# Row maxima in two halves, residual sums ahead of the layer norm, and gated products on GpSimd

## The reference, cut to what matters

```
gate  = q . mean(k of a chunk of 32 tokens); own chunk always, later chunks never
sel   = the 4 best chunks for each token and head
p     = softmax(q.k / sqrt(8)) over the keys of selected chunks, causal
o     = p @ v ;  o * rsqrt(mean(o*o) + 1e-6) * weight * sigmoid(x @ Wg1.T @ Wg2.T)
x1    = layernorm(x + o @ Wo.T)
z     = 2*x1 + shared experts(x1) + sum over 16 experts of gate * (relu(x1@w1+b1) @ w2 + b2)
out   = layernorm(z)
```

## Time and profile before

| | |
|---|---|
| median of 3 runs | 1453.98 us (1453.93 to 1454.67) |
| the profiled execution | 1453.75 us |
| its span, first to last instruction | 1451.7 us |
| PE busy | 1332.4 us, 92% of the span |
| DVE busy | 1087.7 us, 75% |
| ACT busy | 842.7 us, 58% |
| POOL busy | 533.9 us, 37% |

### The profile page before, as it was taken

One profiled execution on the slowest core, in us unless ns is written; L12 is line 12 of the kernel. 1 busy time (PEld: TensorE's weight loads), 2 busy tenths in 40 slices (PEclk: granted clock), 3 DMA queues, 4 the chain that ended last, 5 costly groups with the idle time before them and its releaser, 6 DMA issues.

```text
span 1451.7 us, 29057 instructions
## 1 busy us (share of the span) xinstructions
PE 1332.4 (92%) x10992; PEld 738.7 (51%) x10992; DVE 1087.7 (75%) x2747; ACT 842.7 (58%) x1266; POOL 533.9 (37%) x638
## 2 busy tenths in 40 slices
PE   5677999999998999999999999989999899999597
PEld 3422475535754366534755356543665347553364
DVE  6994688957897578966889578975889668885434
ACT  5406774396735876277743967358762877439121
POOL 3203542254323642245422553235432454225143
PEclk8667999999999999999999999999999999999799
DMA  6001022200321021210222003210112102220031
GB/s 243 16 15 17 16 79 76 52 17 16 104 66 38 30 59 60 74 31 16 82 71 55 16 17 102 71 33 30 60 62 71 31 16 68 73 53 23 13 113 58
DMA packets 52283, 77.81 MB, mean 54 GB/s; under 512 B 6334, under 2 KB 26800, under 8 KB 51888
## 3 DMA queue, kind: packets, MB, share of 16 engines
q1 hardware_dynamic: 52144, 75.96, 18.0%
HBM read 67.02 MB, written 8.65 MB: 52 GB/s over the span
## 4 chain that ended last, share of the span: by engine, by line
PE 61%; DVE 19%; ACT 11%; DVEq 3%; issue 3%; DMA 2%; POOL 1%; SPq 0%; POOLq 0%
PE PS L562 14%; PE PS L574 13%; PE PS L718 8%; ACT UQ L992 7%; PE PS L492 7%; PE PS L509 3%; DVE hr L1163 3%; ACT UK L992 2%; DVE CM L1356 2%; DVEq L1155 2%; PE PS L773 2%; PE PS L413 2%; DVE CM L1275 2%; PE PS L728 2%; PE PS L483 2%
## 5 line engine op out<-in xcount | busy, mean ns | idle before, releaser
L1051 POOL TENSOR_TENSOR hp<-hr,hp 128x512 f16<-128x512 f32 (+1 forms) x200 | 237.1, 1186 | 584.1 <-ACT hp L849 520.0
L1356 DVE TENSOR_REDUCE CM<-PS 128x32 f32<-128x1024 f32 x320 | 376.2, 1218 | 23.2 <-PE PS L492 18.9
L574 PE MATMUL PS<-W,hp 128*128 128x256 f16 (+1 forms) x2400 | 323.2, 274 | 4.6 <-POOL hp L1051 3.6
L562 PE MATMUL PS<-x1T,W 128*128 128x512 f16 (+1 forms) x1200 | 320.6, 385 | 0.0
L840 ACT ACTIVATE hr<-PS,CF 128x512 f32<-128x512 f32 (+1 forms) x200 | 137.2, 686 | 234.3 <-PE PS L562 234.3
L574 PEld LDWEIGHTS PS<-W,hp 128*128 128x128 f16 (+1 forms) x2400 | 216.9, 98 | 96.1 <-issue 34.7
L849 ACT ACTIVATE hp<-hr 128x512 f16<-128x512 f32 (+1 forms) x178 | 112.5, 632 | 169.3 <-DVE hr L1163 156.2
L1163 DVE TENSOR_TENSOR hr<-hr,gB 128x512 f32<-128x512 f32 x176 | 126.2, 717 | 64.9 <-ACT hr L840 58.5
L992 ACT ACTIVATE UK<-PS 128x1024 f32<-128x1024 f32 x160 | 153.0, 1037 | 11.4 <-PE PS L509 11.0
L562 PEld LDWEIGHTS PS<-x1T,W 128*128 128x128 f16 (+1 forms) x1200 | 107.7, 100 | 100.7 <-issue 34.9
L992 ACT ACTIVATE UQ<-PS 128x1024 f32<-128x1024 f32 x160 | 150.9, 1041 | 3.1 <-PE PS L509 1.4
(11 more groups left out here) (150 smaller groups left out, 1793.8 us busy)
## 6 DMA issues: line engine op xcount, KB each, us to landing
gB<-gates SPq DMA_DIRECT2D x64, 256.0 KB, 3.3
gB<-gates SPq DMA_DIRECT2D x32, 224.0 KB, 2.9
gB<-gates SPq DMA_DIRECT2D x32, 192.0 KB, 2.9
gB<-gates SPq DMA_DIRECT2D x32, 160.0 KB, 2.6
xT<-in_xT SPq DMA_DIRECT2D x8, 512.0 KB, 5.8
qET<-rows SPq DMA_DIRECT2D x16, 256.0 KB, 5.2
v<-in_x SPq DMA_DIRECT2D x8, 512.0 KB, 4.1
gB<-gates SPq DMA_DIRECT2D x32, 128.0 KB, 2.9
```

The source lines that it names most:

```text
L562: mm = pe.matmul(PS[0:w, BK_H[c % 2], :], W1[:, a, k, bass.ds(f0, w)], x1T[:, e, k, :], start=(n == 0), stop=(n == 5))
L574: mm = pe.matmul(PS[:, BK_Y + j // 2, (j % 2) * D:(j % 2 + 1) * D], hp[0:w, slot, a, j * P:(j + 1) * P], W2[0:w, e, bass.ds(c, 1), :].rear ...
L1051: nc.gpsimd.tensor_tensor(hp[0:w, slot, 1, :], hr[0:w, slot, :], hp[0:w, slot, 0, :], ALU.subtract).then_inc(pool_hp, 1)
L1356: nc.vector.tensor_reduce(dst, src, AX.X, ALU.max).then_inc(dve_cm, 1)
```

## The change

1. Chunks. The maxima stage takes chunks 11 to 23 and the `up` of chunk 24 (`DEALT` has 91 pieces); the transition as a block of its own is gone. The parts of `down` for chunks 22 (three of four), 23 and 24 stand among the first nine units of the probability stage.
2. Gated products of chunks 11 to 23 are done by POOL, just ahead of its `low`. Chunk 24's relu, gated product and high part are done by DVE after the maxima stage; its `low` stands inside POOL's first causal group.
3. The biased maxima are made in two halves of 16 heads. The first half's four tiles are made in the maxima stage (after the reductions of units 21, 24, 27 and 30), transposed by PE in unit 34, scaled by ACT. The second half's follow after chunk 24's steps on DVE; PE transposes them after unit 8 of the probability stage and DVE scales them.
4. The transfers of selection rows and maxima rows are in two halves too. Unit 0 waits for the first half, unit 20 for the second. The first half is issued by SP ahead of the gate transfer of chunk 24.
5. The output gate's matmuls and tanh stand in the maxima stage, at chunks 14 and 15.
6. Bank pair 2 is first used by unit 10 in place of unit 5, and only after the residual sums have been read; the order of pairs then is 2, 0, 1 throughout.
7. On DVE: scaling of the second maxima, residual sums, copy of the outputs of group 0, then the whole layer norm, without the copy inside.

```
-PAIRS = ((0, 1, 0, 1, 0), (2, 1, 0, 2, 1), (0, 1, 2, 0, 1), (2, 0, 1, 2, 1))
-C_FIRST, C_TOPK, C_MAX, C_BIAS = (0, 3), (3, 11), (11, 22), (22, 25)
+PAIRS = [n % 2 if n < 2 * NU else (2, 0, 1)[(n - 2 * NU) % 3] for n in range(TU)]
+BACK = [next((k for k in range(1, n + 1) if PAIRS[n - k] == PAIRS[n]), 0) for n in range(TU)]
+C_FIRST, C_TOPK, C_MAX, C_LATE = (0, 3), (3, 11), (11, 24), (24, 25)
-DEALT += [(MC - 2, 4), (MC - 2, 5), (MC - 2, 6)]
+DEALT += [(MC, 0), (MC, 1), (MC, 2)]
+AT_SEL, AT_GATE, AT_NEG = (1, 2), (3, 4), 11
...
# SP, in spread_gates(m), for chunk c
+                    if m < B - 1 and c == NC - 1:
+                        bias_rows(m + 1, 0)
...
# PE, after the 40 max units
+                pe.wait_ge(s_rows[0], 64 * (b + 1))
+                unit(0, 0)
+                unit(0, 1)
+                late_down(NC - 3, (1,))
+                unit(0, 2)
+                late_down(NC - 3, (2, 3))
+                unit(0, 3)
+                late_down(NC - 2, (0, 1))
+                unit(0, 4)
+                late_down(NC - 2, (2, 3))
+                unit(1, 0)
+                if m is not None:
+                    pe.wait_ge(s_hid, (m + 1) * NC + 2)
+                outputs(0, 0, 0)
+                unit(1, 1)
+                late_down(NC - 1, (0, 1))
+                unit(1, 2)
+                outputs(0, 0, 1)
+                late_down(NC - 1, (2, 3))
+                unit(1, 3)
+                maxima_rows(BK_H[1], 1)
+                outputs(0, 0, 2)
+                unit(1, 4)
+                outputs(0, 0, 3)
...
# POOL, maxima stage
+                    for c in range(*C_MAX):
+                        gated(m, c, c % 2)
                         low(m, c, c % 2)
...
# DVE
+                        if u in FREE:
+                            maxima(FREE.index(u), 0)
...
+                    nc.vector.tensor_scalar(hr[:, s_last, :], PS[:, BK_H[s_last], :], b1[:, NC - 1:NC], 0.0, ALU.add,
+                                            ALU.max).then_inc(s_hid, 1)
+                    dve.drain()
+                    gated(m, NC - 1, s_last, split=True)
                 for j in range(NT):
+                    maxima(j, 1)
+                dve.wait_ge(pe_neg, 2 * b + 2)
+                nc.vector.tensor_scalar(negT[:, 1, :], PS[0:HALF, BK_H[1], :], 1.0 / UNIT, None, ALU.mult).then_inc(dve_neg, 1)
...
                 if m is not None:
-                    finish(m, lambda: copy_outputs(0))
-                else:
-                    copy_outputs(0)
+                    residual(m)
+                copy_outputs(0)
+                if m is not None:
+                    finish(m)
```

More of the change, by code:

```diff
@@ L98 @@
 UNITS2 = struct.unpack("f", struct.pack("ee", UNIT, UNIT))[0]
+FREE = [u for u in range(TU // 2, MU) if all(part != 2 for _, part in dealt(u - 1))][0:2 * NT:2]
 def gate_pieces(c):
@@ L257, in build @@
         act_neg = sem("act_neg")
-        s_rows = sem("s_rows")
+        dve_neg = sem("dve_neg")
+        s_rows = [sem(f"s_rows{n}") for n in range(2)]
         pe_g1 = sem("pe_g1")
@@ L706, in unit, with late_down @@
+                def late_down(c, parts):
+                    for j in parts if m is not None else ():
+                        down(m, c, c % 2, j)
+                def unit(g, d):
+                    n = g * NU + d
+                    if n < RING:
+                        pe.wait_ge(dve_cm, (b + 1) * TU + n + 1)
+                    if BACK[n]:
+                        pe.wait_ge(act_p, b * TU + n + 1 + RING - BACK[n])
+                    if n == 2 * NU and m is not None:
                         pe.wait_ge(dve_z, 2 * m + 3)
-                    key_unit(g, PAIRS[gs][d], d)
+                    if n == TU // 2:
+                        pe.wait_ge(s_rows[1], 64 * (b + 1))
+                    key_unit(g, PAIRS[n], d)
@@ L942, in turn @@
                             high(m, c, (C_TOPK[0] + u) % 2)
-                for i in range(0, MAX_STEPS):
-                    for u in range(MC):
-                        c = i * MC + C_MAX[0] + u
-                        if m is not None:
-                            relu(m, c, (C_MAX[0] + u) % 2)
-                        if i == 0 and u in (1, 2):
-                            act.wait_ge(pe_sel, 2 * b + u)
-                            nc.scalar.activation(stage_sel[u - 1], PSH[:, BK_H[(c + 1) % 2], :].rearrange("p (q s) -> p q s", q=2),
-                                                 ACT.Copy, scale=-OFF).then_inc(act_sel, 1)
-                        if m is not None:
-                            high(m, c, (C_MAX[0] + u) % 2)
@@ L1107, in causal @@
                     for n, t in enumerate(KORDER):
+                        if g == 0 and n == 1 and m is not None:
+                            for c in range(*C_LATE):
+                                low(m, c, c % 2)
                         if n != 2:
```

234 lines of the change are left out of this document (112 added, 122 removed).

## The result

| | before | after |
|---|---|---|
| median | 1453.95 us (1452.48 to 1454.67, 4 runs) | 1470.18 us (1463.3 to 1472.01, 4 runs) |
| profiled execution, its span | 1453.75, 1451.7 us | 1463.3, 1461.5 us |
| PE, DVE, POOL busy | 1332.4, 1087.7, 533.9 us | 1352.8, 1077.1, 649.6 us |

The ratio is 1.0099, 95% interval 1.0067 to 1.013: slower by 1.0%. I had forecast 1448 (1437 to 1460) and was wrong in sign, and the time is outside the range. The profiled execution is the quickest of the four; the others have spans of 1467.9 to 1470.3 us. Two more executions on record, outside these four, took 1463.27 and 1469.59 us. That spread is a part of the answer.

The account below looks back on a forecast made before the run. TensorE (PE) was taken to set the pace. Per turn +7.2 stage, -11.4 transition, +2.2 first ten units, +1.7 norm made -0.3 us; 1453.75 - 2.4 (seven turns) - 3 (turn 0) = 1448.3 us, range 1437 to 1460.

Parts of the forecast that it names:

- new wait for copy 1: Probability stage: TensorE waits for VectorE's copy of group 1's outputs, behind the norm, just before exponential 18; +1.7 us.
- the gate matmuls: Maxima stage: the output gate's matmuls, moved in, bring TensorE 1.13 us a turn.
- the clock behind a wait: Turns 1 to 7: the prediction has no term for TensorE's clock falling behind a wait.
- the norm's stall: Probability stage: the norm, taken as 5.8 us, delays copy of group 1 and exponential 18; +1.7 us a turn.
- Stage and transition: First max unit to first exponential: +7.2 us of TensorE work in the stage, -11.4 us of transition, a turn.
- GpSimd's products: Maxima stage: gated products on GpSimd take 1.2 us each, fit the slack and cost nothing.
- DVE's relief: Maxima stage: DVE loses 11 gated products of 0.72 us each, 7.9 us a turn.
- First ten units: Start of the probability stage: unit 10 waits for the residual sums, so exponential 10 starts 2.2 us later.
- Turn 0: First turn, without chunks: first exponential 4.7 us earlier, about 1.5 lost again in groups 1 and 2; taken as -3.
- Rival (a): Probability stage: norm and residual sums bite harder, 1.8 us more a turn, about 1461 us; chance 0.26.
- rival B: In e7's own expectations: VectorE partly held TensorE up in the maxima stage; 0.3 to 1 us a turn faster, 1446 to 1451.

Follow-up runs that it names:

- e2: Changed kernel with the output gate's eight matmuls and both tanh back behind the 40 max units: 1481.58 us, ratio 1.0187 to the kernel before.
- e3: Changed kernel with the gated products of chunks 11 to 23 on VectorE again: 1493.86 us, ratio 1.0267 to the kernel before.
- e7: Kernel before with one part of the change alone, the gated products of chunks 11 to 21 on GpSimd: 1449.21 us, ratio 0.9967.
- e4: Changed kernel with the residual sums ahead of the scaling of the second half's maxima on VectorE: 1460.76 us, ratio 1.0047 to the kernel before.
- e5: Changed kernel with the second layer norm left out in turns 1 to 7: 1441.18 us, ratio 0.9906 to the kernel before.
- e1: Changed kernel with keep of group 0 and copy of group 1's outputs ahead of the norm's last four instructions: 1454.85 us, ratio 1.0004 to the kernel before.
- e6: Changed kernel with e4's edit and the norm cut in two, its last four instructions after the copy of group 2: 1447.22 us, ratio 0.995.
- e8: Changed kernel with the edits of e4 and e1 together: 1450.79 us, ratio 0.9975 to the kernel before.
- e12: Changed kernel with unit 17's matmuls issued seven times, ahead of TensorE's wait for the copy of group 1: 1460.1 us, ratio 1.0041 to the kernel before.
- e10: Changed kernel with 14 unneeded transposes put where TensorE waits for the copy of group 1: 1470.12 us, ratio 1.0107 to the kernel before.
- e9: e6 with the norm spread further: statistics, root and last four instructions after the copies of groups 2, 4 and 6: 1459.7 us, ratio 1.0039.
- e11: e6 with the norm in three pieces, after the copies of groups 0, 2 and 4: 1436.32 us, ratio 0.9884 to the kernel before.

## Why the prediction was wrong

*The form was right, the sizes were not.* I had the order of gains and losses: stage and transition shorter, unit 10 later, a new wait for copy 1. Three steps failed. By size in the profiled run: the gate matmuls were priced at 1.13 us and took 2.26 (8 us over seven turns); the clock behind a wait was put at nothing (4.3 us in three turns); the norm's stall was priced at 1.7 us and cost 2.5.

*Stage and transition (the largest failed step):* forecast -4.2 us a turn, measured -2.94. The mis-sized term is the gate matmuls: I took 1.13 us for all eight, each half takes as much, and e2 shows the stage 2.3 us shorter without them. From the first max unit to the first exponential the mean change is -3.16; the other 0.2 us were lost between the heads and the first max unit; the clock falls there in three turns, and what else acts there was not looked for. Seven turns: +8.8 us.

*GpSimd's products:* a product took 1.26 us, forecast 1.2, and PE's `down` waited for POOL only 3.7 us in the whole run, so they cost nothing, as forecast. But I gave them no worth either; e3 shows 3 us a turn in this order, e7 0.5 in the old one. DVE's relief was over-priced (7.9 us; e7 shows 4.2) without effect on the sum.

*First ten units:* forecast +2.2, measured +2.7 at exponential 10. The transposes came 0.6 us later than I had them, and the sums stood behind their scaling; e4 takes 0.77 back. Without the norm 1.9 are left at the turn's end (43.68 against 41.74), so the term was right.

*The norm's stall (failed in size):* I charged 1.7 us at exponential 18; the norm took 6.3 us in place of 5.8 (809.84 to 816.12) and began 0.5 later, and in the undisturbed turns it costs 2.5 (46.2 against 43.7 in e5). I also wrote that later groups were as before. They were only behind the longer wait: as soon as copy 1 was relieved, copy 2 was late (e1, e6, e8). With the term above that is 4.2 us a turn over the mean before (4.5 over its undisturbed turns), against 3.9: +2.2 us in seven turns.

*The clock (a term put at nothing without a reason):* I priced a wait at its own length. Behind it TensorE ran at 1.2 GHz for some us: 1.3, 1.5 and 2.5 us more in three turns, 5.3 in the profiled run. Of the last, 1.0 is the late root of turn 5, so the clock's own part is 1.3 to 1.5 a fall, 4.3 in all. A rival "the new wait costs the clock as well", with 1.3 to 1.5 us in up to seven turns, would have reached from 1450 to 1459. The Trainium skill (TensorE: Matmul & The Clock Gate, section HAM oscillation) says that a TensorE that keeps waiting for data is throttled and starts the next work cold. The traces agree in three turns of seven here and in all seven of e2. The rows had the 0.64 of turn 0 to warn me, and the trace before had two falls of its own.

*Turn 0:* forecast -4.7 and +1.5, measured -4.05 and +0.47.

*The sum:* 1448.3 forecast, + 8.8 stage, + 2.2 unit 10 and norm, + 5.3 clock and late root, - 0.6 turn 0, - 0.7 end = 1463.3, the profiled run's time. The median is 6.9 us above it. The three other runs have a lower mean clock (0.952 to 0.955 against 0.959), which over their spans is an estimated 12 to 21 us more at 1.2 GHz, so more turns with a fall are likely; they have no trace of their own, and that part is inferred. In e12 and e10, which change TensorE's idle time at this place, the mean clock is 0.959 or more in every run.

Rival (a) named 1461 us, close to the profiled run, but that is luck. Its mechanism, the norm and the residual sums, is worth 2.2 us of the 15.0 by which this run missed the forecast, far from the 1.8 us a turn that it had; copy 2 was not late either. The gate matmuls and the clock make up the rest, and no rival had them.

## What to carry to other kernels

When a step is moved ahead of a queue's work, write down what is behind it in that queue and who waits for that; cut a long chain (here a layer norm) into pieces and put each just behind a copy that somebody waits for. Here a wait of the bound engine cost its own length and, where the clock fell behind it, 1.3 to 1.5 us more, so a saving that leaves one such wait behind can be a loss. And look at what GpSimd does at the new place before moving a piece of VectorE's there (e9, e11: the same four instructions, 3.60 or 1.82 us; the kernels differ by 23 us, of which 1.8 us in each of six turns are this, and the rest was not taken apart). And look for the gain where it is: e7's came in rival B's range and at another place.

## What the runs showed of the hardware that I had not expected

- Idle TensorE of 2.47 us ahead of one instruction was followed by a clock of 0.69 and 0.72 (windows of 5 and 6 us) in two turns of the changed kernel and by no fall in four, and by a fall in all seven turns of e2, where another wait of 1.2 us stood some 20 us ahead; 3.43 and 2.12 us (turn 5 of two kernels) by 0.78; 1.16 us never (six turns of e12).
- Two inputs in f32 cost GpSimd 1264 ns, an instruction on the same tile with one f16 input and an f16 output 1189 (the low part, in the page after). The Trainium skill (GPSIMD Engine Reference, Engine selection) advises VectorE for such work; the product is 1.8 times as long there as on VectorE (690 ns), and moving it was right all the same, as VectorE's queue was what TensorE waited for.
- VectorE's 128x256 scale and shift, four times: 1.38 us alone, 1.82 to 2.11 beside GpSimd's selects, 3.60 beside its selects, f16 copies and fills (e9, turns 1 to 6; 1.82 in its turn 7, with selects alone). The Trainium skill (GPSIMD Engine Reference, Specifications) names the shared interface; the size of the loss is these rows'.
- Four matmuls of 8 rows in one row group and one bank take as long (1.13 us) as eight that alternate between two row groups and two banks.
